# Weights loaded first, row counts dropped, and two layers that end a slot later in a graph attention kernel on one core

## The reference, cut to what matters

```python
# layer 0
h = x @ W.T
e = leaky(h @ a_left [:, None] + h @ a_right [None, :]);  e = where(adj == 0, -1e9, e)
x = layernorm(x + softmax(e, axis=-1) @ h)
# layer 1: softmax over axis 1 (columns), then elu
x = layernorm(x + elu(softmax(where(adj > 0, e, -9e15), axis=1) @ h))
# layer 2: h has a bias, softmax over rows again, then elu
x = layernorm(x + elu(softmax(where(adj > 0, e, -1e9), axis=2) @ h))
# layer 3: relations; adj holds only 0 and 1, so one of the four is ever used
x = layernorm(x + adj @ x @ weight[0] + bias)
```

## Time and profile before

| what | value |
|---|---|
| time, median of 3 runs | 482.32 us (481.08 to 482.47) |
| time of the profiled execution | 483.51 us, with a span of 481.7 us between first and last instruction |
| granted TensorE clock, mean | 0.957 of full speed |
| busy share of the span | PE 81%, weight loads 71%, DVE 79%, ACT 75%, POOL 59% |
| instructions | 10006 |

### The profile page before, as it was taken

How to read it: one execution, slowest core, us unless ns; L and a number is a source line. 1 busy time by engine, 2 the same in 40 slices (tenths; PEclk the granted TensorE clock), 3 DMA queues, 4 the chain that set the end, 5 groups by cost and what they waited for, 6 DMA issues and landing times. The chain is left out here.

```text
span 481.7 us, 10006 instructions
## 1 busy us (share of the span) xinstructions
PE 390.6 (81%) x3154; PEld 343.3 (71%) x3161; DVE 380.5 (79%) x1384; ACT 359.3 (75%) x869; POOL 286.5 (59%) x425
## 2 busy tenths in 40 slices
PE   0279999999997987767667788999999959989870
PEld 0279998989996876656657677998999957545440
DVE  0123787878899889999999976788888997888862
ACT  1187687989867879889889886767777775787764
POOL 4033567877774345344353455777777885887883
PEclk9995999999998879999999999999999998999995
DMA  8995045320000000000000000000000000011112
GB/s 201 216 316 119 7 84 84 54 42 2 1 3 1 1 1 1 2 1 1 0 2 1 1 3 0 2 2 1 2 2 0 2 3 0 1 66 67 66 68 89
DMA packets 8759, 18.24 MB, mean 38 GB/s; under 512 B 1280, under 2 KB 2560, under 8 KB 8704
## 3 DMA queue, kind: packets, MB, share of 16 engines
q0 software_dynamic: 2304, 8.39, 9.5%
q1 hardware_dynamic: 2976, 4.52, 2.8%
q10 hardware_dynamic: 3424, 4.66, 2.7%
HBM read 21.76 MB, written 4.19 MB: 54 GB/s over the span
## 5 line engine op out<-in xcount | busy, mean ns | idle before, releaser
L458 PE MATMUL o_ps<-h_scaled,PT 128*128 128x129 f32 (+1 forms) x1536 | 190.2, 284 | 18.5 <-POOL h_scaled L239 15.6
L458 PEld LDWEIGHTS o_ps<-h_scaled,PT 128*128 128x128 f32 x1536 | 182.9, 199 | 21.1 <-issue 18.0
L671 ACT ACTIVATE X<-y,offset,rstd 128x128 f32<-128x128 f32 x256 | 104.8, 480 | 11.8 <-POOL offset L258 11.7
L891 DVE SCALAR_TENSOR_TENSOR PT<-rows_ps,factors,MT 128x512 f32<-128x512 f32 x128 | 89.3, 739 | 0.0
L246 POOL TENSOR_TENSOR var_eps<-mean_var,eps_tile 128x4 f32<-128x4 f32 x64 | 12.9, 201 | 119.7 <-DVE mean_var L965 119.7
L249 POOL TENSOR_TENSOR rstd<-var_eps,neg_half 128x4 f32<-128x4 f32 x64 | 65.2, 1019 | 5.0
L394 PE MATMUL h_ps<-wx,xT 128*128 128x130 f32 x384 | 63.7, 305 | 2.9 <-DVE smax L859 0.5
L394 PEld LDWEIGHTS h_ps<-wx,xT 128*128 128x128 f32 x384 | 54.3, 204 | 12.8 <-issue 11.4
L958 DVE BATCH_NORM_STATS2 stats<-y 128x6 f32<-128x128 f32 x256 | 55.7, 280 | 4.9
L644 ACT ACTIVATE edge<-edge,col_tmp,col_full 128x512 f32<-128x512 f32 x64 | 48.4, 802 | 12.6 <-DVE edge L871 12.5
L239 POOL TENSOR_TENSOR h_scaled<-hx,factors 128x516 f32<-128x516 f32 x32 | 33.6, 1051 | 36.8 <-ACT factors L621 26.4
(11 more groups left out here) (101 smaller groups left out, 682.9 us busy)
## 6 DMA issues: line engine op xcount, KB each, us to landing
MT<-adj_by_j POOLq DMA_DIRECT2D x16, 512.0 KB, 7.3
X<-x SPq DMA_DIRECT2D x16, 256.0 KB, 16.2
out<-X ACTq DMA_DIRECT2D x16, 256.0 KB, 2.0
w_rel<-w SPq DMA_DIRECT2D x1, 256.0 KB, 20.1
wx<-w_by_input ACTq DMA_DIRECT2D x1, 192.0 KB, 3.8
w_back<-w_by_output ACTq DMA_DIRECT2D x1, 192.0 KB, 4.8
bias<-b ACTq DMA_DIRECT2D x1, 64.0 KB, 12.9
bias<-b SPq DMA_DIRECT2D x1, 64.0 KB, 22.9
```

The costliest lines, as they stand in the source:

```text
L458: last = pe.matmul(o_ps[it.b][:, ic, first:1 + D], PT[:, it.b, jc, ic * P:(ic + 1) * P], h_scaled[:, it.b, jc, first:1 + D], start=(jc == ...
L671: last = act.activation(X[:, g, c, :], y[:, b, c, :], ACT.Identity, bias=offset[:, b, c:c + 1], scale=rstd[:, b, c:c + 1])
L891: dve.scalar_tensor_tensor(out=PT[:, it.b, c, :], in0=rows_ps[:], scalar=factors[:, it.b, 1, c:c + 1], in1=m, op0=ALU.max, op1=ALU.mult, * ...
```

## The change

The change has five parts.

1. The ACT queue loads w_back, a_cols and wx first, and only these count in `w_in`; the three transfers for the bias of layer 2 count in `b_in`, for which PE waits in slot -1. POOL waits for `w_in` before its first mask. SP lets x of graph n go only when mask n - 2 has landed, and loads the weights of layer 3 last.
2. The row counts on PE are gone, and with them PE's wait for the mask in `project`. DVE reads empty rows from column 0 of the attention product, which is the sum of the weights, in `row_sums` at(-1). So POOL's mean term and residual of layer 0 move from at(1) to at(-1). DVE now waits for the mask in `weights`, and `flag` moves from at(4) to at(0).
3. The mean of h is one product instead of two, with h laid out in PSUM as 2 x 2 x 130 instead of 4 x 256. `h_mean` has eight buffers instead of two.
4. Layers 0 and 1 end a slot later: y, moments, 1/std and offset are now at(-2) and the normalising at(-3), as layer 2 had them. `attend` waits for y of the item two before, which still reads the same `o_ps` buffer.
5. In layer 1 DVE's y and moments stand between the four edges and the mask products, instead of between the second and third mask product.

```diff
@@ block.sync @@
             for n in range(G):
+                if n >= 2:
+                    sp.wait_ge(sem(f"mask_in{n - 2}"), 16)
                 load_x(item(n))
-                if n == 3:
-                    sp.dma_start(w_rel[:, :, :], w3.rearrange("r d o -> d r o")).then_inc(sem("w_late"), 16)
-                    sp.dma_start(bias3[:, :], b3.partition_broadcast(P)).then_inc(sem("w_late"), 16)
+            sp.dma_start(w_rel[:, :, :], w3.rearrange("r d o -> d r o")).then_inc(sem("w_late"), 16)
+            sp.dma_start(bias3[:, :], b3.partition_broadcast(P)).then_inc(sem("w_late"), 16)
-        W_IN = 16 * 6
+        W_IN, B_IN = 16 * 3, 16 * 3
@@ block.gpsimd @@
-                if at(1) and at(1).l != 1:
+                if at(-1) and at(-1).l == 0:
+                    mean(at(-1))
+                    add_residual(at(-1))
+                if at(1) and at(1).l == 2:
                     mean(at(1))
                 if at(-1) and at(-1).l == 2:
                     elu_low(at(-1))
-                if at(-2) and at(-2).l == 2:
+                if at(-2):
                     find_rstd(at(-2))
                     find_offset(at(-2))
-                if at(-1) and at(-1).l != 2:
-                    find_rstd(at(-1))
-                if at(-1) and at(-1).l != 2:
-                    find_offset(at(-1))
-                if at(1) and at(1).l == 0:
-                    add_residual(at(1))
                 if at(1) and at(1).l == 1:
                     scale_h(at(1))
+            pool.wait_ge(sem("w_in"), W_IN)
             for g in range(8 + FIRST):
                 load_mask(item(g))
@@ block.tensor: project_layer, project, attend, attention_slot @@
-                    for e in range(2):
-                        last = pe.matmul(h_mean_ps[:, e, :], x_sum[:, b:b + 1].broadcast_to([P, P]),
-                                         wx[:, l, e * 64:(e + 1) * 64], start=True, stop=(l != 2))
+                    last = pe.matmul(h_mean_ps, x_sum[:, b:b + 1].broadcast_to([P, P]), wx[:, l, 0:D],
+                                     start=True, stop=(l != 2))
...
-                if it.l == 0:
-                    pe.wait_ge(sem(f"mask_in{it.g}"), 16)
...
-                if it.l == 0:
-                    for ic in range(C):
-                        for jc in range(C):
-                            last = pe.matmul(h_ps[:, ic, 130:131], MT[:, it.g, jc, ic * P:(ic + 1) * P],
-                                             ones_bf[:, 0:1], start=(jc == 0), stop=(jc == C - 1))
...
                 pe.wait_ge(sem("h_scaled"), it.done)
+                if it.done > 2 and item(it.done - 3).l < 2:
+                    pe.wait_ge(sem("y_sum"), it.done - 2)
...
+                if n == -1:
+                    pe.wait_ge(sem("b_in"), B_IN)
+                    pe.matmul(o_ps[1][:, 0, 0:2], bias2_col[:, 0:1].broadcast_to([P, P]), a_cols[:, 2, :],
+                              start=True, stop=True).then_inc(sem("b2_ps"), 1)
@@ block.scalar @@
-            act.dma_start(wx[:, :, 0:D], w_in).then_inc(sem("w_in"), 16)
             act.dma_start(w_back[:, :, :], w_out).then_inc(sem("w_in"), 16)
             act.dma_start(a_cols[:, :, :], a_in).then_inc(sem("w_in"), 16)
+            act.dma_start(wx[:, :, 0:D], w_in).then_inc(sem("w_in"), 16)
...
-                    if it.l > 0 or it.g >= 2:
-                        act.wait_ge(sem("mean_raw"), halves(it) - 2)
+                    if it.l > 0 or it.g >= 8:
+                        act.wait_ge(sem("mean_raw"), halves(it) - 8)
...
-                if at(-2) and at(-2).l < 2:
-                    take_norm(at(-2))
-                if at(-3) and at(-3).l == 2:
+                if at(-3):
                     take_norm(at(-3))
...
-                if at(4) and at(4).l == 0:
-                    flag(at(4))
+                if at(0) and at(0).l == 0:
+                    flag(at(0))
@@ block.vector @@
             def row_sums(it):
                 dve.wait_ge(sem("att"), it.done)
+                if it.l == 0:
+                    dve.tensor_scalar(empty_row[:, it.g, :], o_ps[it.b][:, :, 0], 0.0, None, ALU.is_equal)\
+                        .then_inc(sem("empty_row"), 1)
...
-                if at(-1) and at(-1).l != 1:
+                if at(-2) and at(-2).l == 0:
+                    take_out(at(-2))
+                if at(-1) and at(-1).l == 2:
                     take_out(at(-1))
-                if at(-2) and at(-2).l == 2:
+                if at(-2) and at(-2).l > 0:
                     add_elu(at(-2))
+                if at(-2):
                     finish(at(-2))
                 if at(1):
                     weights(at(1), (0, 1))
-                if at(-2) and at(-2).l == 2:
+                if at(-2):
                     aggregate(at(-2))
-                if at(-1) and at(-1).l == 1:
-                    add_elu(at(-1))
-                if at(-1) and at(-1).l != 2:
-                    finish(at(-1))
                 if at(1):
                     weights(at(1), (2, 3))
...
-                if at(-1) and at(-1).l != 2:
-                    aggregate(at(-1))
```

More of the change, by code:

```diff
@@ L23 @@
 LAYERS = 3
-S1, S2, DEG = 129, 130, 131
+S1, S2 = 129, 130
 FIRST, ALL_STEPS = -4, 2 + G * (LAYERS + 1)
@@ L71, in build @@
         hx = sb("hx", [P, 4, C, 132])
-        h_mean = sb("h_mean", [P, 2, D])
+        h_mean = sb("h_mean", [P, 8, D])
         h_scaled = sb("h_scaled", [P, 2, C, 132])
@@ L128, in build, with h_chunk_ps, halves_of @@
         xT_ps = pb("xT_ps", [P, N])
-        h_ps = pb("h_ps", [P, C, 256])
+        h_ps = pb("h_ps", [P, 2, 512])
         rows_ps = pb("rows_ps", [P, N])
         o_ps = [pb(f"o_ps{b}", [P, C, 256]) for b in range(2)]
-        h_mean_ps = h_ps[:, 2:4, 132:196]
-        smax_ps = h_ps[:, 0:2, 132:196]
+        h_all_ps = h_ps[:, :, 0:260].rearrange("p k (c w) -> p k c w", c=2)
+        smax_ps, h_mean_ps = h_ps[:, 0, 260:260 + P], h_ps[:, 1, 260:260 + D]
+        def h_chunk_ps(c, width):
+            return h_ps[:, c // 2, (c % 2) * 130:(c % 2) * 130 + width]
         sums_ps = (xT_ps, rows_ps)
         block = ctx.enter_context(nc.Block())
+        def halves_of(chunks):
+            return chunks.rearrange("p (k c) w -> p k c w", k=2)
         def pipeline(slot, begin, end, items):
@@ L215, in mean @@
                 pool.tensor_tensor(mean_term[:, it.b, :, :],
-                                   h_mean[:, it.b, :].unsqueeze(1).broadcast_to([P, C, D]),
+                                   h_mean[:, it.m, :].unsqueeze(1).broadcast_to([P, C, D]),
                                    empty_row[:, it.g, :].unsqueeze(2).broadcast_to([P, C, D]),
@@ L369, in _ @@
             for l in range(LAYERS):
-                pe.matmul(xT_ps[:, 2 * l:2 * l + 2], w_back[:, l, :], a_cols[:, l, :], start=True, stop=True)
-            pe.matmul(xT_ps[:, 6:8], bias2_col[:, 0:1].broadcast_to([P, P]), a_cols[:, 2, :],
-                      start=True, stop=True).then_inc(sem("wa_ps"), 1)
+                last = pe.matmul(xT_ps[:, 2 * l:2 * l + 2], w_back[:, l, :], a_cols[:, l, :], start=True, stop=True)
+            last.then_inc(sem("wa_ps"), 1)
             pe.wait_ge(sem("ident"), 1)
@@ L547, in redo @@
                         for c in range(C):
-                            last = pe.matmul(h_ps[:, c, 0:D], xT[:, 0, c * P:(c + 1) * P], w_rel[:, r, :],
+                            last = pe.matmul(h_chunk_ps(c, D), xT[:, 0, c * P:(c + 1) * P], w_rel[:, r, :],
                                              start=True, stop=True)
@@ L747, in redo @@
                         if l != 1:
-                            act.activation(h_mean[:, 0, :].rearrange("p (e d) -> p e d", e=2), h_mean_ps, ACT.Copy,
+                            act.activation(h_mean[:, 0, :], h_mean_ps, ACT.Copy,
                                            scale=1.0 / N).then_inc(sem("re_h_mean"), 1)
-                        act.copy(hx[:, 0, :, 1:131], h_ps[:, :, 0:130]).then_inc(sem("re_hx"), 1)
+                        act.copy(halves_of(hx[:, 0, :, 1:131]), h_all_ps).then_inc(sem("re_hx"), 1)
                         act.wait_ge(sem("re_smax"), k)
@@ L1121, in redo @@
                         dve.wait_ge(sem("re_split_hi"), n)
-                        dve.tensor_tensor(rest[:, 0, :, :], h_ps[:, :, 0:D], split[:, 0, 0, :, :], ALU.subtract)\
+                        dve.tensor_tensor(halves_of(rest[:, 0, :, :]), h_all_ps[:, :, :, 0:D],
+                                          halves_of(split[:, 0, 0, :, :]), ALU.subtract)\
                             .then_inc(sem("re_split_rest"), 1)
```

45 lines of the change are left out of this document (23 added, 22 removed).

## The result

The changed kernel takes 494.68 us (median of 4 runs, 493.98 to 495.95) against 481.70 us of the kernel before, run beside it (480.12 to 482.47): a ratio of 1.030, 95% interval 1.026 to 1.034. It is slower by 13 us, where the prediction said 4 us faster with 467 to 488 as its range. The profiled execution took 493.98 us, with a span of 492.2; before, the span was 481.7.

What follows compares the result with a forecast made beforehand. It took PE to bound layers 0 and 2 and DVE layer 1; -15.5 - 8.3 + 1 + 23.7 - 2.2 - 2.6 = -3.9 on 483.51 us gave 479.6, carried over to 478, range 467 to 488.

Steps and rivals of the forecast that it cites:

- the term of layer 1: Slots 18 to 30: ACT's exponent waits for the late y, a loop of 10.5 us for 8.68; +23.7 us.
- q_rows to first edge 0.63: Layer 1, first piece of ACT's loop: 0.63 us from q_rows to DVE's first edge, in a sum of 10.45.
- Slots 13 to 17, +1: Slot 15 becomes 9.4 us by ACT, slots 16 and 17 some 8.8; +1 us (0 to +4).
- PE's loop, "8.4": Layer 1: PE also waits for y before attend, but its loop is shorter than ACT's, 8.4 us.
- rival B: Layer 1: PE's clock falls in every slot, making slots 11.1 us, term +31.5, total 486; chance 0.18.
- Rival C: Layer 1: POOL blocks DVE's mask products, DVE's loop takes 10.7 us, time 481 (479 to 483); chance 0.15.
- Rival A: Layer 1: ACT's wait doesn't bind, slots stay at DVE's 8.7 us, time 455 (450 to 460); chance 0.12.
- Start and layer 0: Start: earlier weights, attend(0) at 27.5 us instead of 43.16, -15.5; layer 0, slots 1 to 12: 6.2 us for 6.89, -8.3.
- a sign of being wrong: Slots -2 to 2: the forecast is wrong if x arrives later than needed, with PE waiting for X.
- the split of layer 2's bias at 0: Bias2's split keeps cover or order: 0; uncovered, it and similar costs stay below 2 us (seven small DVE instructions).
- Layer 2, -2.6: Slots 33 to 44: the mean's 0.56 us on PE becomes 0.34, 12 x -0.22 = -2.6 us (-4 to -1).

Runs made afterwards that it cites:

- e1_elu_two: Changed kernel with two buffers instead of one for ELU's exponent, so ACT waits for y of two items before; 477.44 us, ratio 0.992.
- e2_y_first: Changed kernel, but in layer 1 DVE makes y of item n-2 ahead of the column bias and four edges; 466.52 us, ratio 0.970.
- e4_l1_as_before: Changed kernel, but layer 1 ends in the slot in which it ended before the change; 469.27 us, ratio 0.977.
- e3_bias_early: Changed kernel, but in layer 1 DVE computes the column bias of item n+2 at the end of slot n; 487.11 us, ratio 1.014.
- e6_pe_busy: Changed kernel, but PE writes the transposed x six times instead of once in slots with layer 1's edges; 492.71 us, ratio 1.026.
- e12_all_y_first: Changed kernel with layer 1's y, and in slots 15 to 17 layer 0's last y, ahead of column bias and edges; 462.23 us, ratio 0.961.
- e13_elu_busy: Changed kernel with both two buffers for ELU's exponent and PE kept busy by repeated transposes ahead of attend; 458.18 us, ratio 0.952.
- e5_start_only: Kernel before the change with only the new order of transfers at the start; 475.48 us, ratio 0.991.
- e7_two_means: Changed kernel, but the mean of h again in two products of 64 columns (four in layer 2); 497.70 us, ratio 1.035.

## Why the prediction was wrong

**The step that failed** is the term of layer 1, "13 x (10.5 - 8.68) = +23.7": the mechanism was right and its size off. ACT does wait behind y, and the loop is the one described; e1_elu_two, e2_y_first and e4_l1_as_before each take it away. The term came out at +30.7, mostly because the piece "q_rows to first edge 0.63" doubled to 1.26. That number was read where the bias wasn't blocked. When ACT's wait makes hx, DVE's reciprocal, h_scaled and the bias come together, POOL's product starts 0.26 us ahead of the bias and holds it 0.60 us longer. e3_bias_early shows it: 10.44 us without the block (10.35 in most slots), against 10.45 worked out. That is 7.9 of the 30.7 us. That the average fell so near the sum is in part chance, since the steady slot is 0.1 shorter and the last one 1.0 longer.

**Slots 13 to 17, +1.** The second mis-sized term, +6.0. It took slot 15 from ACT at 9.4 and slots 16 and 17 at 8.8. The 8.8 is PE's loop behind the late y with 1.1 us for it (2.65 + 1.1 + 0.1 + 4.9), so that the wait was in it. What failed is its 4.9 us for attend and what follows, taken at the fast clock and with the bias unblocked. Slots 15 to 17 are each 10.8 to 11.0 us long, and in slot 15 attend takes 5.45 us for 3.81 and the bias 0.84 us for 0.21, together 2.3 more. e6_pe_busy, where the clock alone is cured, has them at 9.4; e12_all_y_first, with y ahead of the edges, at as much.

**PE's loop, "8.4".** Wrong as well, though it didn't decide in slots 18 to 30: it is 10.0 us in most slots (e1_elu_two), since attend was put in at its fast length. With the fast attend it is as worked out: 8.38 us in e13_elu_busy. That the low clock would recur rival B had right, and the argument against it, that PE fills its gaps at the low clock so that the clock comes back, fails: it comes back in every slot and falls again in most. As the cause of layer 1's time B is refuted all the same, by e6_pe_busy.

**Rival C** named the right mechanism, VectorE against GpSimd, at the wrong instructions. The first mask product does take 1.09 us beside the elu_exp addition, and DVE has 28 us of idle time in the stage. The block that counted was on a 4-element instruction. **Rival A** fell with the 3.54 us wait.

**Start and layer 0** came out as worked out, -14.5 and -8.5 for -15.5 and -8.3, but the start by other means than told. In the changed kernel the weights are there at 5.92 us (7 was taken) and attend(0) begins at 30.9, not at 27.5:

```profile
5.92 1.35 PEld L378 LDWEIGHTS xT_ps<-a_cols,w_back 128*128 128x128 f32 x6 [5.92 <-DMA wx<-w_by_input]
...
30.89 1.28 PE L459 MATMUL o_ps<-h_scaled,PT 128*128 128x129 f32 x10
```

It then runs at the full clock, about 3.7 us where the earlier trace rows had 5.95, which gives back 2.2. And e5_start_only puts half of it on the transfers. The other half belongs to the rest of the change (row counts, flag, buffers of the mean, the layer 0 end) and to the clock in slot 0. The traces place it, 3.5 us ahead of PE's projection in slot 0 and 3.7 behind it, where the clock is low. How much each part of the change would give alone no run shows.

The prediction named a sign of being wrong here: PE waiting for x in slots -2 to 2. PE does wait 4.62 us in slot -2 of the changed kernel, for x of item 2, which SP holds back until mask 0 has landed:

```profile
19.12 1.09 PE L386 MATMUL xT_ps<-ident,X 128*128 128x128 f32 x4 [4.62 <-DMA X<-x]
```

It also put the split of layer 2's bias at 0. In the changed kernel its seven DVE instructions (27.59 to 29.23 us) stand ahead of the maximum of slot 0, for which PE waits 1.47 us. So attend(0) came 3.4 us later than worked out, and the term was nearly met because the full clock gave back 2.2.

**Layer 2, -2.6** came to -0.1. PE's 82.03 of 83.80 us in the earlier trace rows was read as the bound, and it was only one of two. In the changed kernel PE has less to do and waits:

```profile
345.20 0.62 PE L446 MATMUL rows_ps<-ident,factors 128*128 128x128 f32 x4 [0.28 <-DVE PT L895]
```

The slot runs in the loop over the single rows_ps (last mask product, rows, maximum, DVE's slot) at 6.97 us as before. That DVE's loop sets it is read from this wait and from e7_two_means, whose longer mean leaves the slot at 6.97; no run shortened DVE's part.

**Sum.** Layer 1's term stayed below its upper bound of +32, and alone it would have given 485, inside the range. Slots 13 to 17 went over theirs (+6.0 for +4), slots 33 to 44 too (-0.1 for -1), and all three err to the same side.
